# New order tables for a macaron block (feed-forward, state space layer, feed-forward): one position for each piece of a batch item

## What is computed

```python
x = x + 0.5 * ffn(layernorm(x))
x = x + ssm(layernorm(x))
x = x + 0.5 * ffn(layernorm(x))

def ffn(x):   # hidden size 768
    gate = x @ wg.T; up = x @ wu.T          # integer weights, scaled by 1/127
    return (silu(gate) * up) @ wd.T

def ssm(x):   # E = 256 channels, n = 16 states, r = 64
    z = x @ W_z.T; params = x @ W_params.T
    dt = softplus(params[..., :r] @ W_dt.T + b_dt);  C = params[..., r + n:]
    u = silu(causal_conv4(x))
    A = -exp(A_log); a = exp(dt * A); b = (a - 1) / A
    h[t] = a[t-1] * h[t-1] + b[t-1] * u[t-1]          # per channel and state
    return ((sum_n C[n] * h[n] + u * D) * silu(z)) @ W_out.T
```

## Time and profile before

| | |
|---|---|
| Time, median of 3 runs | 2578.41 us (2577.72 to 2578.85) |
| Profiled execution: its time, its span | 2578.04 us, 2576.0 us |
| DVE busy | 2287.3 us (89%) |
| PE busy | 2290.1 us (89%) |
| POOL busy | 2074.4 us (81%) |
| ACT busy | 1984.9 us (77%) |
| Mean granted TensorE clock | 0.933 of full speed |
| First scan starts | 135.52 us after the span's start |
| Items 1 to 14, first scan of 1 to first scan of 15 | 272.39 to 2373.96 us |
| Last scan starts | 2499.67 us |

### The profile page before, as it was taken

One profiled execution on the slowest core, in us unless ns is written; L12 is line 12 of the kernel. 1 busy time (PEld: TensorE's weight loads), 2 busy tenths in 40 slices (PEclk: granted clock), 3 DMA queues, 4 the chain that ended last, 5 costly groups with the idle time before them and its releaser, 6 DMA issues.

```text
span 2576.0 us, 28487 instructions
## 1 busy us (share of the span) xinstructions
PE 2290.1 (89%) x9220; PEld 1382.1 (54%) x9220; DVE 2287.3 (89%) x2294; ACT 1984.9 (77%) x2830; POOL 2074.4 (81%) x1286
## 2 busy tenths in 40 slices
PE   6877799899998989999898999999899999988478
PEld 3443455556465555646555564655556565555245
DVE  2189999999999999999999999999999999999981
ACT  4668787887878788787877878787787878776643
POOL 2367988888798888879888888988888898888772
PEclk9887999999999999999999999999999999998689
DMA  2133334334343433434343343434334343433430
GB/s 73 34 118 120 131 116 130 128 118 139 108 147 116 131 130 117 139 108 147 121 132 121 119 139 107 148 121 133 122 119 139 107 147 122 133 114 115 140 115 17
DMA packets 112025, 307.97 MB, mean 120 GB/s; under 512 B 11201, under 2 KB 45314, under 8 KB 111874
## 3 DMA queue, kind: packets, MB, share of 16 engines
q1 hardware_dynamic: 111874, 306.13, 36.3%
HBM read 288.27 MB, written 17.83 MB: 119 GB/s over the span
## 4 chain that ended last, share of the span: by engine, by line
PE 50%; ACT 19%; DVE 13%; issue 10%; POOL 7%; DMA 1%; DVEq 0%; SPq 0%; POOLq 0%; ACTq 0%
PE work L543 19%; PE work L531 12%; DVE g_bank L977 7%; PE work L582 6%; ACT ring L781 5%; POOL acc L856 4%; PE work L511 4%; DVE ring L1008 4%; ACT normed L624 4%; PE work L553 2%; ACT L611 2%; PE work L560 2%; PE work L590 2%; ACT xt_lo L662 1%; PE work L597 1%
## 5 line engine op out<-in xcount | busy, mean ns | idle before, releaser
L856 POOL TENSOR_TENSOR acc<-acc,ring 128x1024 f32<-128x1024 f32 x512 | 1211.0, 2365 | 175.3 <-DVE ring L1008 154.8
L977 DVE TENSOR_TENSOR_SCAN g_bank<-du_bank,ring 128x1024 f32<-128x1024 f32 x512 | 1174.6, 2294 | 29.9 <-ACT du_bank L768 15.8
L543 PE MATMUL work<-wd_t,hid 128*128 128x256 f32 x3072 | 691.7, 386 | 22.2 <-DVE hid L948 18.5
L1008 DVE SCALAR_TENSOR_TENSOR ring<-g_bank,inv_a,ring 128x1024 f32<-128x1024 f32 x512 | 654.9, 1279 | 11.3
L543 PEld LDWEIGHTS work<-wd_t,hid 128*128 128x128 f32 x3072 | 596.3, 194 | 117.9 <-DVE hid L948 21.3
L781 ACT ACTIVATE ring<-dt,a_coef 128x1024 f32<-128x1024 f32 x512 | 548.0, 1138 | 1.5 <-DVE g_bank L977 0.2
L825 POOL TENSOR_TENSOR hid<-hid,sil 128x512 f32<-128x512 f32 x192 | 244.6, 1274 | 136.3 <-ACT hid L683 136.3
L531 PE MATMUL work<-xt_hi,wg_t 128*128 128x512 f16 x768 | 311.1, 405 | 42.7 <-ACT xt L649 15.7
L611 ACT ACT_TABLE_LOAD x257 | 329.7, 1283 | 4.6
L531 PE MATMUL work<-xt_lo,wg_t 128*128 128x512 f16 x768 | 310.8, 405 | 0.0
L531 PE MATMUL work<-xt_hi,wu_t 128*128 128x512 f16 x768 | 302.4, 394 | 5.3 <-ACT sil L675 5.2
(11 more groups left out here) (90 smaller groups left out, 2829.2 us busy)
## 6 DMA issues: line engine op xcount, KB each, us to landing
ring<-c_rows SPq DMA_DIRECT2D x512, 512.0 KB, 3.7
x_in<-L_attn_x SPq DMA_DIRECT2D x32, 512.0 KB, 4.6
out<-x_fin SPq DMA_DIRECT2D x32, 512.0 KB, 4.0
c_rows<-params SPq DMA_DIRECT2D x32, 32.0 KB, 3.4
ring<-L_ffn_w_gate SPq DMA_DIRECT2D x1, 768.0 KB, 5.8
ring<-L_ffn_w_up SPq DMA_DIRECT2D x1, 768.0 KB, 7.2
ring<-L_ffn_w_down SPq DMA_DIRECT2D x1, 768.0 KB, 10.5
wz_t<-L_attn_W_z SPq DMA_DIRECT2D x1, 256.0 KB
```

The lines of the kernel that those rows point to most:

```text
L543: last = pe.matmul(dst[:, j * E:(j + 1) * E], hid[:, K.unit[f, bt, c, m] % HIDS, t:t + P], wd_t[:, m, :], start=(m == 0), stop=(m == HM - 1))
L856: nc.gpsimd.tensor_tensor(acc[bt % 2][:, h, :], acc[bt % 2][:, h, :], cg[:, slot, :], ALU.add).then_inc(S["summed"], 1)
L977: scan = nc.vector.tensor_tensor_scan(g_bank[:], du_bank[:], decay[:, a, :], 0.0, ALU.add, ALU.mult)
L1008: nc.vector.scalar_tensor_tensor(cg[:, k, :], g_bank[:], inv_a[:, h, s:s + 1], spread[:, k_c, :], ALU.mult, ALU.mult).then_inc(S["weighted ...
```

## The change

`AT`, `PACE` and `LAG` go. `ROW` has one number for every piece of an item: 12 for each of `ga`, `si`, `up`, 32 for each of `scan`, `cm`, `bc`, `ex`. `HEAD` replaces those of the pieces of item 0 that stand ahead of its scans, `TAIL` those of the pieces of item 15 that stand behind. The phases are gone, so an `ex` may stand alone among silus. The computation of each piece is the same, and so is their number, but for the table loads: by the new list ACT changes its table 285 times where it was 257, and 18 times where it was 16 in each item from 1 to 13.

```diff
-AT = {
-    "scan0": [0.67, -0.01], "cm": [0.75], "bc": [-4.95], "ld": [-57.56, -40.12], "ln1": [-41.46, -36.46],
...
-def phase(t, start):
-    return CYCLE * ((t - start) // CYCLE) + start
+ROW = {
...
+    "up1": [-34.159, -31.142, -29.993, -29.456, -28.651, -28.408, -25.055, -24.192, -22.517, -22.244, -21.291,
+        -20.209],
...
+def row_events(b):
+
+    for f in (1, 2, 3):
+        for c in range(NC):
+            for kind in ("ln", "lr", "ls", "lx", "T", "Te") + (("Ts", "Tl") if f != 2 else ()):
+                yield f"{kind}{f}", (kind, f, b, c)
...
 def schedule():
     out = []
...
     for b in range(B):
-        t0 = SLOTS * b
...
+        seen = {}
+        for name, ev in row_events(b):
+            table = HEAD if b == 0 and name in HEAD else TAIL if b == B - 1 and name in TAIL else ROW
+            i = seen[name] = seen.get(name, -1) + 1
+            out.append((round(SLOTS * b + table[name][i], 3), len(out), ev))
     return [ev for _, _, ev in sorted(out)]
@@ in the PE program
                 elif kind in ("ga", "up"):
-                    if kind == "ga" and m == 0:
+                    if m == 0:
 
                         wait(pe, "free", ("T", 1 if f == 1 else 3, bt, c, EH - 1))
```

More of the change, by code:

```diff
@@ L66 @@
 PROWS = C_ROW + N
-AT = {
[6 rows of a table removed]
-}
-PACE = {
-    "gu1": 0.732, "gu2": 1.087,
-}
-LAG = {
[8 rows of a table removed]
-}
-def phase(t, start):
-    return CYCLE * ((t - start) // CYCLE) + start
+ROW = {
[60 rows of a table added]
+    "gate": [19.727, 32.263],
+    "scan": [0.473, 0.907, 1.407, 3.334, 3.51, 5.343, 5.932, 7.743, 9.271, 9.34, 9.992, 10.665, 12.478, 13.411,
+        13.731, 14.826, 15.673, 17.327, 19.46, 19.744, 19.947, 20.646, 22.015, 22.359, 23.68, 24.914, 25.549, 26.359,
+        28.392, 28.808, 30.379, 31.434],
+    "cm": [0.508, 1.241, 2.372, 3.398, 4.678, 5.801, 6.446, 8.509, 9.304, 9.827, 10.462, 11.722, 13.1, 13.612,
+        14.524, 15.275, 15.995, 17.887, 19.491, 19.924, 20.061, 20.911, 22.072, 23.377, 24.366, 24.978, 26.248,
+        27.161, 28.765, 29.713, 30.841, 31.859],
+    "bc": [-6.792, -6.789, -3.961, -2.628, -2.493, -0.819, 1.129, 1.142, 1.22, 1.311, 2.443, 3.884, 6.404, 6.612,
+        6.924, 7.211, 7.773, 9.335, 9.419, 12.673, 12.674, 13.46, 14.532, 14.942, 15.011, 15.458, 15.869, 16.486,
+        17.118, 22.136, 22.787, 24.875],
+    "ex": [-2.038, -0.421, -0.411, 0.101, 2.866, 3.721, 3.896, 4.503, 4.766, 5.107, 5.535, 6.057, 11.117, 11.372,
+        12.407, 12.731, 12.77, 12.88, 12.983, 14.718, 18.141, 18.578, 18.617, 20.823, 21.842, 22.292, 22.704, 22.879,
+        24.082, 28.089, 28.396, 28.901],
+    "op": [35.407, 36.428, 38.789, 39.029],
+    "rc": [35.378, 35.561, 36.43, 38.134],
+    "ra": [33.47, 34.623, 36.383, 38.384],
+}
@@ new lines @@
+TAIL = {
[20 rows of a table added]
+}
+def row_events(b):
[3 more added lines that the diff above has]
+                yield f"{kind}{f}", (kind, f, b, c)
+    for f in (1, 2):
+        for c in range(NC):
+            for m in range(HM):
+                for kind in ("ga", "si", "up") + (("sc", "hp") if m in POOLED else ("sh",)):
+                    yield f"{kind}{f}", (kind, f, b, c, m)
+            for jp in range(2):
+                yield f"dn{f}", ("dn", f, b, c, jp)
+                yield f"rs{f}", ("rs", f, b, c, jp)
+                if f == 1:
+                    yield "rp", ("rp", b, c, jp)
+    for c in range(NC):
+        for kind in ("ld", "pm", "pe", "cw", "st"):
+            yield kind, (kind, b, c)
+    for h in range(EH):
+        for c in range(NC):
+            for kind in ("cv", "us", "z", "zs", "dt", "da", "dl", "dp", "rm", "ai"):
+                yield kind, (kind, b, h, c)
+    for kind in ("u0", "dt0"):
+        yield kind, (kind, b)
+    for p in range(EH):
+        for kind in ("d", "db", "gate"):
+            yield kind, (kind, b, p)
+        for s in range(N):
+            for kind in ("scan", "cm", "bc", "ex"):
+                yield kind, (kind, b, s, p)
+    for jp in range(2 * NC):
+        for kind in ("op", "rc", "ra"):
+            yield kind, (kind, b, jp)
@@ L106, in schedule @@
 def schedule():
     out = []
-    def at(t, *ev):
-        out.append((t, len(out), ev))
-    def put(t0, name, i, *ev):
-        at(t0 + AT[name][i], *ev)
-    def after(t0, name, lag, i, *ev):
-        at(t0 + AT[name][i] + LAG[lag][i], *ev)
-    def rows(t0, f, b):
-        for c in range(NC):
-            put(t0, f"ln{f}", c, "ln", f, b, c)
-            for kind in ("lr", "ls", "lx", "T", "Te") + (("Ts", "Tl") if f != 2 else ()):
-                after(t0, f"ln{f}", f"{kind}{f}", c, kind, f, b, c)
```

102 lines of the change are left out of this document (41 added, 61 removed), and 91 rows, old and new, of tables (AT, LAG, ROW, TAIL).

## The result

| | before | after |
|---|---|---|
| Time, median of 4 runs each | 2578.06 us (2575.96 to 2578.85) | 2478.38 us (2477.59 to 2478.42) |
| Profiled execution's span, mean clock | 2576.0 us, 0.933 | 2476.6 us, 0.948 |
| DVE, PE, POOL, ACT busy | 89, 89, 81, 77% | 92, 91, 84, 81% |

A forecast was written before the change was run, and what follows sets the result against it. DVE was taken as the bound, PE only 38 us behind. Gains of 53 (items 1 to 14), 12 (head), 4 (items 0 and 15) and 1.7 (tail) sum to 70.7 us, from 2578.04 to 2507 us; range 2478 to 2560.

The forecast's parts named there:

- the signs: What the new profile should show: first scan at 123 to 125 us, items of 146.3 us, 285 loads, root and rm waits under 5.
- The waits as a sum: Items 1 to 14: of DVE's 82.9 us of waits, 20 stay and 63 go.
- Root and shift: Second layernorm's shift, each item: root ready 7.3 us behind the scan, 2 us slack; 24 of 27.8 us of wait go.
- Accumulator start: The four ai of each item: DVE's wait for PE's rm falls from 17.8 us to 3.
- Against it, 10 us: Items 1 to 14: ai's operation on two SBUF tiles lasts longer beside POOL's accumulation, costing 10 us, at most 28.
- Table loads: ACT: 28 more loads, 36 us, covered by its idle time and costed at nothing; without cover up to 36 us.
- Head, ends, tail: Gains outside items 1 to 14: head 12 us, items 0 and 15 4 us, tail 1.7 us.
- the first three steps: Head: down projection group in PE's idle time (4 us), dt products ahead of a convolution (1.5), z ahead of three rm (1.5).
- step (a): Head: one down projection group of 6 us fills PE's idle time around the transposes; gain 4 us.
- The first (waits move): PE and ACT hold each other up, DVE keeps two thirds or more of its waits: 2540 to 2568 us; chance 0.27.
- The second: Item border: up product late behind a down projection group; 2539 us with old lateness, 2591 at 6.5 us; chance 0.04, as slower.
- The third: Lock: shifts directly behind a cm held some 2.3 us longer by the accumulation it releases: 2618 us; chance 0.03.

The follow-up runs named there:

- e8: e2 with POOL's product of block m = 2 also moved, behind the root instead of ahead of the accumulation: 2576.37 us.
- e2: Kernel before, with the second layernorm's first-chunk statistics and root moved behind the cm of state 9, its shift behind that of state 10: 2590.1 us.
- e10: Changed kernel with the second layernorm's first-chunk statistics and shift, and POOL's product, back in their old order at this place: 2518.05 us.
- e4: Changed kernel with two more table loads on ACT in each item, ahead of the copy of u's first column: 2502.11 us.
- e7: Changed kernel with the last rm ahead of a gate product on PE and half 0's second ai ahead of its first on DVE: 2454.58 us.
- e3: Kernel before, with the cm of state 11 of half 1 directly behind its scan, ahead of the product and four accumulator starts: 2628.85 us.
- e5: Changed kernel with the 512 decays back at their old positions, four together, and 257 table loads: 2665.07 us.
- e6: Changed kernel with the shift of the first layernorm's second chunk moved behind the cm of state 13 of half 1: 2467.43 us.
- e9: e7 with the last up product of the second feed-forward also moved on PE, directly behind its gate product: 2452.17 us.
- e12: e9 with two shifts also moved: the first layernorm's second-chunk one, and the third layernorm's first with its dependent rows: 2453.96 us.

## Why the prediction was right or wrong

**The time.** 71 us were forecast and 100 came. The measured 2478.38 us lie 0.4 us above the lower end of the range, 2478, which is less than the runs differ among themselves: that the range holds the time is luck, and 0.02 stood on what is below it. Of the signs, the root's wait, the number of loads and the absence of waits for a decay came; the `rm` wait (14.5 us, not under 5) and the mean of `ai`'s second operation (1210 ns, not over 1257) did not, and the first scan (121.86) and the item (144.6) were better than said.

**What bounds the kernel.** Right in the main. DVE has the most busy time, and what could be had lay first in its waits: 82.9 us of them in the middle are now 18.8. But DVE was hardly the path before. The chains that ended last, by engine, from the pages of before and after:

```profile
PE 50%; ACT 19%; DVE 13%; issue 10%; POOL 7%; DMA 1%; DVEq 0%; SPq 0%; POOLq 0%; ACTq 0%
DVE 45%; PE 27%; issue 16%; ACT 11%; POOL 1%; DMA 0%; DVEq 0%; SPq 0%; ACTq 0%; POOLq 0%
```

Before, the path of the last result ran over PE and ACT, the suppliers, for 69% of the span; only the new order makes DVE the longest part of it. Such a chain is one path among some that are nearly as long, but it fits what e8 showed, that one wait of DVE taken away does not shorten the old order.

**The waits as a sum.** Right: 20 were to stay, 18.8 did. In their parts less so: root 0 (3 kept), up products 4.0 (9), du_bank 0 (5), `rm` 14.5 (3).

**Root and shift.** Right by its own working: ready 7.3 us behind the scan, slack 1.9 us. That an edit of this one place alone would bring these 24 us is refuted by e2 and e8, in the old order: it brought -12 and 0. The forecast named the place and its chain, and it needs what the other lists do around it (e10: 39 us).

**Accumulator start.** Wrong in size. It was argued that PE would come to `rm` with less behind it. e4 shows that lateness of ACT arrives at just this place, and e7 that the order of PE's own list decides: with one `rm` ahead of a gate product the wait falls to 3.8 us.

**Against it, 10 us: the failed term.** The middle's busy time of DVE was to grow by 10 us at `ai`; it fell by 12.7. The 22.7 us between the two are nearly all of the 24.8 by which the middle was missed, DVE's idle time is the other 2. Two parts. The sum of the durations of DVE's instructions fell from 2087.2 to 2082.1 us: the ten operations with two SBUF inputs take 7.7 us an item together where they took 8.1. The lock that was priced does exist at the fourth `ai` (1.73 us in the mean, 1.0 before), but the `ai` of half 0 and chunk 0, the first in the old list and the second in the new, had 1.76 and now has 1.05. I looked at what one place would meet and not at what the old place already paid. The other 7.6 us are overlap: where an instruction is independent of the one ahead it starts some 0.08 us before that one's end, while a dependent one starts 0.04 behind. In the middle there are 1249 such starts where there were 1141, and 101.4 us of overlap for 93.7. Of the 108 more, 41 come from places between scan and cm that were empty: a scan and a cm stand directly behind one another 537 times, where it was 578. Most of the others come with the waits that went, since what has waited starts without overlap: DVE stood idle for over 0.06 us ahead of 40 instructions, where it was 104. So a wait that goes gives, by this count, some 0.08 us more than its length. In item 8 cm and scan with nothing between are 1.32 us apart (1302.61, 1303.93) and 1.79 with a product between (1306.27, 1308.06), so such a product costs 0.47 us, and 0.60 behind another piece. No row of the forecast had this.

**Table loads.** Right for the 28 of this change, since no wait for a decay came, and ACT's busy time in the middle rose by 29.0 us, no more than 28 loads of the earlier trace rows are. As a rule it was too easy: ACT's idle time as a share was no cover for two loads more at another point (e4). The Trainium skill, "ScalarE: Activation LUTs", section on what ACT_TABLE_LOAD costs, gives 1380 ns of drain for each switch beside the load. The activation behind the load of 118.41 starts at 119.70, again 1.29 us after it, and ahead of all 285 loads ACT was idle for 5.0 us together, so neither trace shows that part.

**Head, ends, tail.** Right: 13.7, 6.4 and 1.6 us for 12, 4 and 1.7. The steps of the head hold too: the down projection ends at 71.74 where it ended at 76.07 (4.3 us for 4), the first eviction of `z` starts at 112.14 where it started at 120.75 (8.6 for the 7 of the first three steps), and 5.0 us come behind it, for 5. In the head PE's first group of the down projection fills the wait for the transposes, as in step (a), and du_bank's copy starts at 120.76 where it started at 134.41; PE, then ACT:

```profile
60.24 5.45 PE L621 MATMUL work<-wd_t,hid 128*128 128x256 f32 x24 [0.78 <-DVE hid L1026]
65.53 1.04 PE L586 MATMUL work<-ident,normed 128*128 128x128 f32 x8
66.40 5.34 PE L621 MATMUL work<-wd_t,hid 128*128 128x256 f32 x24
```

```profile
118.41 1.28 ACT L689 ACT_TABLE_LOAD   x1
119.70 1.15 ACT L859 ACTIVATE ring<-dt,a_coef 128x1024 f32<-128x1024 f32 x1
120.76 1.01 ACT L846 ACTIVATE du_bank<-du 128x1024 f32<-128x1024 f32 x1
```

**Rivals.** The first (waits move) did not come in the whole change. In the old order it came in e8 wholly and in e3 for the larger part; in e2 the waits fell by 9 us in sum, and the lock took more than that. The second did not come; its reserve of 0.9 us was measured as 0.7. The third is real where DVE follows a wait for POOL (e2) or starts behind POOL's accumulation (the shift at 1404.38), not at the shifts behind a cm that it named: those start first, and four of the six take 0.15 us in the mean, such as that at 1317.27.

**Left open.** What the single moves behind the other waits are worth was not tried: of the waits that went, only the root's was undone in the new order (e10), not the places of the up products (wait 28.6 to 4.0 us) or of du_bank's copy (8.7 to 0). e10 brings 18 us of these two back by the root's place alone; the rest is argued from the two lists. Why e5 costs 186 us in its parts was not followed; PE is busy 86 us more in its middle than in the changed kernel's, at a mean granted clock of 0.93 for 0.97, and no run tells what that clock has in it. Whether an order without any lock can be had was tried three times (e6, e9, e12), and not reached.

## What to carry to other kernels

When a hand-made order is replaced as a whole, its edits are not additive: the same move was worth 39 us in one order and nothing in the other, and the early loads, the single decays and the moved pieces pay only together. Price a move by what its old place paid as well as by what the new one may pay, for each engine that shares a resource with it. An engine's idle share is no reserve at a given point; read there who waits for the next thing in its list.
